# Attention slots: the value matmuls placed straight behind the second score pair

## The chip, the cores and the metric

The kernel runs on one core of a Trainium2 chip. The metric is device time in microseconds (us), the median of several executions; lower is better. TensorE (PE in the profile), VectorE (DVE), ScalarE (ACT), GpSimd (POOL) and the DMA queue of SyncE (SP) each take their own instructions in order; they meet at semaphores that the kernel sets and waits for by hand.

## The reference

`x` has 4 batches of 512 tokens of 128 channels. One transformer block with 16 heads of 8 channels, values equal to keys, and a mixture of 8 experts, of which each token takes 2:

```python
q = (x @ Wq + bq).reshape(B, N, H, Dh).transpose(0, 2, 1, 3)
k = (x @ Wk + bk).reshape(B, N, H, Dh).transpose(0, 2, 1, 3)
v = k
attn = jnp.einsum('bhnd,bhmd->bhnm', q, k) * scale
attn = jax.nn.softmax(attn, axis=-1)
out = jnp.einsum('bhnm,bhmd->bhnd', attn, v)
...
x = x + _L0_attn_ref(_layernorm(x, axis=-1), ...)
x = x + _L0_ffn_ref(_layernorm(x, axis=-1), ...)
```

## The kernel before

The four batches `b` go through one after the other. The attention of a batch is a loop over 16 slots `s`. A slot treats one group of four heads (`s // 4`) and one quarter of 128 keys (`s % 4`). After batches 1, 2 and 3 comes a loop over steps, one for each block of 128 expert rows (`up`, `gelu`, `down`); batches 1, 2 and 3 have a 17th slot for the last values.

Four kinds of work stand in TensorE's queue in a slot:

- `score_max` (L1066): one matmul of 512 columns that writes the scores of 128 queries of one head into one of two PSUM buffers, SM0 and SM1 in turn. VectorE takes their row maximum (`row_max`, L802). These maxima are made well ahead of the slot that uses them. A matmul of number m waits for the maximum of number m - 2, which read the same buffer (semaphore `sm_max`). A slot has 4 of them in batches 0 and 1 (5 in the first four slots, none from slot 11 of batch 1), 3 in batch 2, 2 in batch 3 up to slot 9. The steps have two each.
- `score_pair` (L1106): two matmuls into half of ST, which ScalarE turns into exponentials in `probs` (L699). A slot has two pairs. A pair waits for the exponentials of the pair before the last.
- `values` (L1118): four matmuls, one for each head, side by side on 32 columns of the array each, from `probs` of the slot before into AV. It waits for the exponentials of that slot, which the second pair has already waited for; at the first quarter of a group also for ScalarE's copy of AV (`av_done`, L691).
- a job in the PSUM buffer MISC (`fill_misc`): it waits until the job before it has been emptied (`misc_free`). Each engine that empties jobs has them at a fixed place of its own queue. VectorE empties x (turned input, L820), pr (projection, L778), q (turned queries, L797), out (turned attention output, L826 to L833), lg (logits) and rk (ranks); ScalarE empties k (turned keys), qr (turned queries with their row maxima, L603), x2 and xg (turned expert rows).

The jobs of the slots, apart from qr:

```python
0: {1: ("x", 1), 2: ("pr", 1, 0), 3: ("pr", 1, 1), 5: ("k", 1, 0), 6: ("out", 0, 0), 7: ("k", 1, 1),
    8: ("q", 1, 0), 9: ("q", 1, 1), 10: ("out", 0, 1), 14: ("out", 0, 2)},
1: {0: ("x", 2), 1: ("out", 0, 3), 2: ("pr", 2, 0), 3: ("x2", 0), 4: ("lg", 0), 5: ("pr", 2, 1), 6: ("rk", 0),
    8: ("out", 1, 0), 9: ("k", 2, 0), 10: ("out", 1, 1), 11: ("k", 2, 1), 12: ("q", 2, 0), 13: ("q", 2, 1),
    14: ("out", 1, 2), 15: ("xg", 0)},
2: {6: ("out", 2, 0), 10: ("out", 2, 1), 14: ("out", 2, 2), 15: ("xg", NQ)},
3: {6: ("out", 3, 0), 10: ("out", 3, 1), 14: ("out", 3, 2), 15: ("xg", 2 * NQ)},
```

The qr jobs are in slots 3, 7 and 11 of every batch and in slot 15 of batch 0: in batches 0 and 1 at the end of the slot, behind the last `score_max`, and in batches 2 and 3 ahead of the first pair.

VectorE's queue in a slot is: the first two row maxima, its part of the job, the other row maxima, and in some slots further work (layer norm moments and normalizing, choice of experts, `gate_weights`, `finish`), which stands at the end of the slot. ScalarE's is: the two exponentials, its part of the jobs, splitting of weights, the copy of AV.

Of the kernel before, what the change touches and what calls it, by code (L numbers as in the profile page):

```python
# [20 lines left out]
def preln_attention_moe(nc, x, wq, bq, wk, bk, w_gate, W1, b1, W2, b2, out):  # L21
# [3 lines left out]
    B, N, C = x.shape  # L25
    H, Dh = 16, C // 16
    E, _, F = W1.shape
    T = N // P
    G = H // 4
# [10 lines left out]
    with ExitStack() as ctx:  # L40
# [179 lines left out]
        def blocks_after(b):  # L220

            return range(0) if b == 0 else range(NB * (b - 1), NB * (b if b < B - 1 else B))

        def steps(b):

            return len(blocks_after(b)) + LAG if b else 0
# [21 lines left out]
        def slots(b):  # L248

            return range(4 * G if b == 0 else 4 * G + 1)  # L250

        def late_qr(b):

            return b <= 1
# [11 lines left out]
        def qr_of_slot(b, s):  # L266

            if s in QR:
                return ("qr", b, QR.index(s))
            if b == 0 and s == 4 * G - 1:  # L270
                return ("qr", 1, 0)
            return None

        def misc_of_slot(b, s):

            job, qr = IN_SLOT[b].get(s), qr_of_slot(b, s)
            return [j for j in ((job, qr) if late_qr(b) else (qr, job)) if j is not None]
# [744 lines left out]
        def _(pe):  # L1022
# [32 lines left out]
            def score_max(b, m):  # L1055

                if m % 32 == 0 or (b == 0 and m == LEAD):
                    pe.wait_ge(km_in[m // 32], 64 * (b + 1))
                if b == 0 and m == LEAD:
                    pe.wait_ge(qT_done, 2)  # L1060
                if b >= 1 and m % 32 == 0:
                    pe.wait_ge(misc_free, misc_no["q", b, m // 32] + 1)
                if SM_N * b + m >= LEAD + 2:
                    pe.wait_ge(sm_max, SM_N * b + m - 1)
                h = m // 4
                pe.matmul(SM[m % 2][:, :], qT0[:, b % 2, h // 4, P * (m % 4):P * (m % 4) + P], kTm[:, b % 2, h // 4, h % 4, :],  # L1066
                          start=True, stop=True).then_inc(sm_full, 1)
# [24 lines left out]
            def score_pair(b, s, pr):  # L1092

                g, c = s // 4, s % 4
                n = PAIRS * b + 2 * s + pr
                if n >= 2:
                    pe.wait_ge(exp_done, n - 1)
                if s == 0 and b >= 2:
                    if pr == 0:
                        pe.wait_ge(gelu_done, NB * (b - 1))  # L1100
                    else:
                        pe.wait_ge(yev_done, NQ * (b - 1))
                if c == 0:
                    pe.wait_ge(misc_free, misc_no["qr", b, g] + 1)
                for k in (2 * pr, 2 * pr + 1):
                    mm = pe.matmul(ST[:, n % 2, k % 2, :], kTm[:, b % 2, g, k, P * c:P * c + P], qT1[:, g % 2, :],  # L1106
                                   start=True, stop=True)
                mm.then_inc(st_full, 1)

            def values(u):  # L1110

                b, s = divmod(u, 4 * G)
                g, c = s // 4, s % 4
                if c == 0 and u >= 4:
                    pe.wait_ge(av_done, u // 4)
                pe.wait_ge(exp_done, 2 * u + 2)
                for j in range(4):
                    last = pe.matmul(AV[32 * j:32 * j + 32, :], v_aug[:, b % 2, c, 4 * g + j, :],  # L1118
                                     probs[:, (2 * u + j // 2) % 4, j % 2, :], start=(c == 0), stop=(c == T - 1))
                last.then_inc(av_step, 1)  # L1120
# [34 lines left out]
            def pick_expert(v):  # L1155

                f, j = v // NB, v % NB
                if j == 0:
                    pe.wait_ge(ex_done, f + 1)
                expert[v] = pe.value_load(exp_i[0:1, f, j:j + 1], min_val=0, max_val=E - 1)  # L1160

            def up(v):

                gq, j = group_of(v), v % NB % 4
                pe.wait_ge(w_in[v % RW], 16 * (v // RW + 1))
                if j == 0:
                    pe.wait_ge(misc_free, misc_no["xg", gq] + 1)
                if v >= 2:
                    pe.wait_ge(gelu_done, v - 1)
                dst, wb = UP[v % 2], wblk[:, v % RW, :]  # L1170
                pe.matmul(dst, wb[:, 2 * F:WB], sel[:, :, :].rearrange("p c n -> p (c n)"), start=True, stop=False)  # L1171
                for c in range(HC):
                    col = dst[:, P * c:P * c + P]
                    pe.matmul(col, wb[:, P * c:P * c + P], xgT[:, gq % 2, j, 0, :], start=False, stop=False)  # L1174
                    pe.matmul(col, wb[:, P * c:P * c + P], xgT[:, gq % 2, j, 1, :], start=False, stop=False)  # L1175
                    last = pe.matmul(col, wb[:, F + P * c:F + P * c + P], xgT[:, gq % 2, j, 0, :],  # L1176
                                     start=False, stop=(c == HC - 1))
                last.then_inc(up_full, 1)
# [29 lines left out]
            def fill_misc(job):  # L1208

                pe.wait_ge(misc_free, misc_no[job])  # L1210
                if job[0] == "x":
                    last = turn_x(job[1], MISC)
                if job[0] == "pr":
                    pe.wait_ge(misc_free, misc_no["x", job[1]] + 1)
                    project(2 * job[2], MISC)
                    last = project(2 * job[2] + 1, MISC)
                if job[0] == "k":
                    last = turn_k(job[1], job[2], MISC16)
                if job[0] == "q":
                    last = turn_q(job[1], job[2], MISC16)  # L1220
                if job[0] == "qr":
                    last = turn_qr(job[1], job[2])
                if job[0] == "out":
                    last = turn_out(job[1], job[2])
                if job[0] == "xg":
                    last = turn_xg(job[1])
                if job[0] == "x2":
                    last = turn_x2(job[1])
                if job[0] == "lg":
                    last = logits(job[1])  # L1230
                if job[0] == "rk":
                    last = rank_tokens(job[1])
                last.then_inc(misc_full, 1)
# [21 lines left out]
            for b in range(B):  # L1255
                for s in slots(b):
                    sm = sm_slot[b, s]
                    for bb, m in sm[0:1]:
                        score_max(bb, m)
                    if not late_qr(b) and s in QR:  # L1260
                        fill_misc(qr_of_slot(b, s))
                    if s < 4 * G:
                        score_pair(b, s, 0)
                    for bb, m in sm[1:2]:
                        score_max(bb, m)
                    if s < 4 * G:
                        score_pair(b, s, 1)
                    for bb, m in sm[2:3]:
                        score_max(bb, m)
                    for job in misc_of_slot(b, s):  # L1270
                        if job[0] != "qr":
                            fill_misc(job)
                    if s >= 1 or b == 1:
                        values(4 * G * b + s - 1)
                    for bb, m in sm[3:]:
                        score_max(bb, m)
                    if late_qr(b) and qr_of_slot(b, s) is not None:
                        fill_misc(qr_of_slot(b, s))
                todo = blocks_after(b)
                if b >= 1:  # L1280
                    pe.wait_ge(exp_done, PAIRS * (b + 1))
                for i in range(steps(b)):
                    for v in todo[i:i + 1]:
                        pick_expert(v)
                    sm = sm_step[b, i]
                    for bb, m in sm[0:1]:
                        score_max(bb, m)
                    for v in todo[i:i + 1]:
                        up(v)
                    for job in misc_of_step(b, i):  # L1290
                        fill_misc(job)
                    for bb, m in sm[1:2]:
                        score_max(bb, m)
                    if i >= LAG:
                        for v in todo[i - LAG:i - LAG + 1]:
                            down(v)
# [20 lines left out]
```

## Time and profile before

| what | value |
| --- | --- |
| median of 3 executions | 431.66 us (430.49 to 433.51) |
| the profiled execution | 433.75 us, its span 432.0 us |
| TensorE busy | 365.1 us, 85% of the span |
| VectorE busy | 251.6 us, 58% |
| ScalarE busy | 245.3 us, 57% |
| GpSimd busy | 124.5 us, 29% |
| slots of batches 0 and 1 | about 29 to 169 us of the span |
| slots of batch 2 | about 214 to 262 us |
| slots of batch 3 | about 303 to 344 us |

A matmul of 512 columns is shown with a duration of 0.38 us, but the next one can start 0.22 us after it; the duration holds the way through the array. The hardware profiler's times are of one execution; those of the table's first line are of three others.

### The profile page before, as it was taken

The numbers are of one execution on the slowest core, as the hardware profiler recorded it, in microseconds if no ns is written. First come the engines' busy times: TensorE is split into PE (matmuls) and PEld (weight loads), VectorE is DVE, ScalarE is ACT, GpSimd is POOL, SyncE is SP. The second block draws the span as 40 slices with busy tenths as digits, with TensorE's granted clock in tenths as the row PEclk, the third lists the DMA queues.
The fourth block names the chain that finished last, engine by engine and source line by source line (L and its number), as shares of the span: only waits on it lengthen the run. The fifth ranks groups of instructions, "written<-read, shape, count | busy, mean of one in ns | idle before, by whom it ended". The sixth has DMA issues, their size and how long they took to land. (4 is left out here: it accounts for less than half of the span.)

```text
span 432.0 us, 8187 instructions
## 1 busy us (share of the span) xinstructions
PE 365.1 (85%) x2858; PEld 203.3 (47%) x2858; DVE 251.6 (58%) x602; ACT 245.3 (57%) x322; POOL 124.5 (29%) x119
## 2 busy tenths in 40 slices
PE   6764998978787889899999799999899989899910
PEld 3311333322242334788723236788232379789910
DVE  5798777888878736875677877855555052000202
ACT  1423378786764778336487587333889944454410
POOL 5994112230041620203660000260420025107042
PEclk9655799999998999999999999999999999999975
DMA  5968002000000037232381001152720023576321
GB/s 169 313 174 247 2 0 50 1 2 0 27 0 0 31 101 252 85 135 67 113 275 44 24 2 57 56 189 73 231 92 24 2 112 138 168 256 222 114 78 49
DMA packets 43875, 42.92 MB, mean 99 GB/s; under 512 B 3314, under 2 KB 33082, under 8 KB 43836
## 3 DMA queue, kind: packets, MB, share of 16 engines
q1 hardware_dynamic: 41788, 38.20, 27.1%
q0 software_dynamic: 2048, 4.20, 3.3%
q8 instruction: 25, 0.41, 0.4%
q14 instruction: 14, 0.11, 0.1%
HBM read 11.58 MB, written 11.01 MB: 52 GB/s over the span
## 5 line engine op out<-in xcount | busy, mean ns | idle before, releaser
L802 DVE TENSOR_REDUCE q_aug<-SM 128x1 f16<-128x512 f32 x240 | 158.4, 689 | 52.3 <-PE SM L1066 50.6
L699 ACT ACTIVATE probs<-ST 128x1024 f32<-128x1024 f32 x128 | 124.7, 1023 | 53.0 <-PE ST L1106 52.4
L1066 PE MATMUL SM<-kTm,qT 128*128 128x512 f16 x240 | 93.7, 396 | 22.3 <-DVE q_aug L802 20.8
L1106 PE MATMUL ST<-qT,kTm 128*128 128x512 f16 x256 | 77.8, 392 | 7.2 <-ACT qT L603 4.4
L626 ACT ACTIVATE w<-ST 128x512 f32<-128x512 f32 x60 | 35.8, 597 | 77.5 <-PE ST L1176 76.1
L1118 PE MATMUL AV<-probs,v_aug 128*32 128x512 f32 x512 | 69.1, 614 | 0.3 <-ACT probs L699 0.3
L1066 PEld LDWEIGHTS SM<-kTm,qT 128*128 128x128 f16 x240 | 23.4, 99 | 97.3 <-DVE q_aug L802 72.2
L1192 PE MATMUL ST<-w 128*128 x480 | 66.6, 282 | 0.0
L1192 PEld LDWEIGHTS ST<-w 128*128 128x128 f32 x480 | 58.3, 192 | 3.1
L523 POOL DMA_INDIRECT w<-ys,pos x32 | 32.5, 1014 | 64.3 <-issue 44.5
L1175 PE MATMUL ST<-xgT,wblk 128*128 128x128 f16 x240 | 43.3, 219 | 0.0
L1174 PE MATMUL ST<-xgT,wblk 128*128 128x128 f16 x240 | 43.3, 219 | 0.0
L1176 PE MATMUL ST<-xgT,wblk 128*128 128x128 f16 x240 | 43.3, 219 | 0.0
L1106 PEld LDWEIGHTS ST<-qT,kTm 128*128 128x128 f16 x256 | 23.4, 100 | 38.2 <-ACT probs L699 14.3
L442 POOL TENSOR_TENSOR rstd<-ve,neg_half 128x4 f32<-128x4 f32 x8 | 8.2, 1031 | 113.4 <-DVE ve L759 113.3
L511 POOL DMA_INDIRECT xs<-x2s,pos x32 | 31.6, 989 | 22.5 <-DVE pos L884 13.6
L905 DVE SCALAR_TENSOR_TENSOR x<-w,wgt,x 128x128 f32<-128x128 f32 x16 | 4.5, 345 | 54.2 <-DMA w<-ys,pos 54.2
L1175 PEld LDWEIGHTS ST<-xgT,wblk 128*128 128x128 f16 x240 | 23.5, 98 | 7.1
L1174 PEld LDWEIGHTS ST<-xgT,wblk 128*128 128x128 f16 x240 | 23.5, 98 | 3.2
L1176 PEld LDWEIGHTS ST<-xgT,wblk 128*128 128x128 f16 x240 | 23.5, 98 | 0.0
L1171 PE MATMUL ST<-sel,wblk 128*128 128x512 f16 x60 | 22.7, 379 | 0.8 <-DMA wblk<-wpk 0.3
L1118 PEld LDWEIGHTS AV<-probs,v_aug 128*32 128x32 f32 x512 | 10.3, 109 | 19.2 <-issue 12.9
(146 smaller groups left out, 397.2 us busy)
## 6 DMA issues: line engine op xcount, KB each, us to landing
wblk<-wpk SPq DMA_DIRECT2D x60, 288.0 KB, 2.8
xs<-xg SPq DMA_DIRECT2D x4, 960.0 KB, 9.0
xg<-xs SPq DMA_DIRECT2D x12, 256.0 KB, 3.2
ys<-w SPq DMA_DIRECT2D x12, 256.0 KB, 2.3
w<-L_ffn_W SPq DMA_DIRECT2D x1, 2048.0 KB, 11.2
kTm<-kT SPq DMA_DIRECT2D x32, 64.0 KB
xt<-L_attn_x SPq DMA_DIRECT2D x4, 256.0 KB, 6.8
out<-x SPq DMA_DIRECT2D x4, 256.0 KB, 2.2
```

The source lines that it names most:

```text
L511: pool.indirect_dma_start(out=xs[b], out_offset=bass.IndirectOffsetOnAxis(ap=pos[:, b, r, t:t + 1], axis=0), in_=x2s[:, t, :, :].rearrange ...
L523: pool.indirect_dma_start(out=yg[:, t, r, :], out_offset=None, in_=ys[f], in_offset=bass.IndirectOffsetOnAxis(ap=pos[:, f, r, t:t + 1], ax ...
L626: act.activation(hf[:, v % HR, :], UP[v % 2], ACT.Gelu, scale=1.0 / WSCALE).then_inc(gelu_done, 1)
L699: act.activation(probs[:, n % 4, :, :], ST[:, n % 2, :, :], ACT.Exp, scale=SCALE).then_inc(exp_done, 1)
L802: dve.tensor_reduce(q_aug[:, b % 2, m % 4, m // 4, 24:25], SM[m % 2][:, :], AX.X, ALU.max, negate=True).then_inc(sm_max, 1)
L1066: pe.matmul(SM[m % 2][:, :], qT0[:, b % 2, h // 4, P * (m % 4):P * (m % 4) + P], kTm[:, b % 2, h // 4, h % 4, :], start=True, stop=True).t ...
L1106: mm = pe.matmul(ST[:, n % 2, k % 2, :], kTm[:, b % 2, g, k, P * c:P * c + P], qT1[:, g % 2, :], start=True, stop=True)
L1118: last = pe.matmul(AV[32 * j:32 * j + 32, :], v_aug[:, b % 2, c, 4 * g + j, :], probs[:, (2 * u + j // 2) % 4, j % 2, :], start=(c == 0), ...
L1174: pe.matmul(col, wb[:, P * c:P * c + P], xgT[:, gq % 2, j, 0, :], start=False, stop=False)
L1175: pe.matmul(col, wb[:, P * c:P * c + P], xgT[:, gq % 2, j, 1, :], start=False, stop=False)
L1176: last = pe.matmul(col, wb[:, F + P * c:F + P * c + P], xgT[:, gq % 2, j, 0, :], start=False, stop=(c == HC - 1))
L1192: last = pe.matmul(dst, hf[:, v % HR, P * c:P * c + P], w2[:, bass.ds(expert[v], 1), P * c:P * c + P].rearrange("p a n -> p (a n)"), start ...
```

## The change

In the slots, `values` is called straight behind the second `score_pair`, ahead of the third `score_max` and of the job. Nothing else is edited; waits, semaphores and the queues of the other engines stay as they are. In slots without a job it moves ahead of the third `score_max` alone; in batch 3, which has at most two, ahead of the job alone.

```diff
                     if s < 4 * G:
                         score_pair(b, s, 1)
+                    if s >= 1 or b == 1:
+                        values(4 * G * b + s - 1)
                     for bb, m in sm[2:3]:
                         score_max(bb, m)
                     for job in misc_of_slot(b, s):
                         if job[0] != "qr":
                             fill_misc(job)
-                    if s >= 1 or b == 1:
-                        values(4 * G * b + s - 1)
                     for bb, m in sm[3:]:
                         score_max(bb, m)
```

TensorE's queue in slot 9 of batch 0 (job q, `L1051`) and the first rows of slot 10, before:

```order
L1066 MATMUL SM0<-kTm,qT0 128x512
L1106 MATMUL ST<-qT1,kTm 128x512 x2
L1066 MATMUL SM1<-kTm,qT0 128x512
L1106 MATMUL ST<-qT1,kTm 128x512 x2
L1066 MATMUL SM0<-kTm,qT0 128x512
L1051 MATMUL MISC<-ident16,q_aug 128x128 x8
L1118 MATMUL AV<-probs,v_aug 32x512 x4
L1066 MATMUL SM1<-kTm,qT0 128x512
L1066 MATMUL SM0<-kTm,qT0 128x512
```

And the same place after the change:

```order
L1066 MATMUL SM0<-kTm,qT0 128x512
L1106 MATMUL ST<-qT1,kTm 128x512 x2
L1066 MATMUL SM1<-kTm,qT0 128x512
L1106 MATMUL ST<-qT1,kTm 128x512 x2
L1118 MATMUL AV<-probs,v_aug 32x512 x4
L1066 MATMUL SM0<-kTm,qT0 128x512
L1051 MATMUL MISC<-ident16,q_aug 128x128 x8
L1066 MATMUL SM1<-kTm,qT0 128x512
L1066 MATMUL SM0<-kTm,qT0 128x512
```

The values stood between the job and the fourth matmul into SM; now they stand between the second pair and the third, and the job is followed by the fourth.

TensorE's queue in slots 4 and 5 of batch 2 (three maxima, no job), before, from the second pair of slot 4 to that of slot 5:

```order
L1106 MATMUL ST<-qT1,kTm 128x512 x2
L1066 MATMUL SM0<-kTm,qT0 128x512
L1118 MATMUL AV<-probs,v_aug 32x512 x4
L1066 MATMUL SM1<-kTm,qT0 128x512
L1106 MATMUL ST<-qT1,kTm 128x512 x2
L1066 MATMUL SM0<-kTm,qT0 128x512
L1106 MATMUL ST<-qT1,kTm 128x512 x2
```

And after the change:

```order
L1106 MATMUL ST<-qT1,kTm 128x512 x2
L1118 MATMUL AV<-probs,v_aug 32x512 x4
L1066 MATMUL SM0<-kTm,qT0 128x512
L1066 MATMUL SM1<-kTm,qT0 128x512
L1106 MATMUL ST<-qT1,kTm 128x512 x2
L1066 MATMUL SM0<-kTm,qT0 128x512
L1106 MATMUL ST<-qT1,kTm 128x512 x2
```

The third matmul into SM, which stood ahead of the values, now stands directly ahead of the first of the next slot.

## Rows read from the trace of the kernel before

**Rows 1.** The page's costliest groups: busy, mean ns | idle before, releaser

```profile
L802 DVE TENSOR_REDUCE q_aug<-SM 128x1 f16<-128x512 f32 x240 | 158.4, 689 | 52.3 <-PE SM L1066 50.6
```

**Rows 2.** Time line, batch 0, from slot 10's second SM matmul: start us, us, engine, line

```profile
80.46 0.39 PE L1066 MATMUL SM<-kTm,qT 128*128 128x512 f16 x1
...
80.69 0.59 PE L1106 MATMUL ST<-qT,kTm 128*128 128x512 f16 x2
...
81.12 0.38 PE L1066 MATMUL SM<-kTm,qT 128*128 128x512 f16 x1
...
81.34 0.60 PE L1126 MATMUL MISC<-ident,avs 128*128 128x128 f32 x4
...
81.87 1.07 PE L1118 MATMUL AV<-probs,v_aug 128*32 128x512 f32 x8
81.97 0.26 DVE L826 RECIPROCAL rden<-MISC 128x16 f32<-128x16 f32 x1 [0.37 <-PE MISC L1126]
...
82.80 1.28 DVE L802 TENSOR_REDUCE q_aug<-SM 128x1 f16<-128x512 f32 x2
...
82.86 0.39 PE L1066 MATMUL SM<-kTm,qT 128*128 128x512 f16 x1
...
83.63 0.38 PE L1066 MATMUL SM<-kTm,qT 128*128 128x512 f16 x1 [0.38 <-DVE q_aug L802]
```

**Rows 3.** Time line, slots 12 and 13 of batch 0, no job

```profile
88.70 0.38 PE L1066 MATMUL SM<-kTm,qT 128*128 128x512 f16 x1
...
89.01 1.06 PE L1118 MATMUL AV<-probs,v_aug 128*32 128x512 f32 x8
...
90.01 0.61 PE L1066 MATMUL SM<-kTm,qT 128*128 128x512 f16 x2
...
90.44 1.29 DVE L802 TENSOR_REDUCE q_aug<-SM 128x1 f16<-128x512 f32 x2 [0.62 <-PE SM L1066]
...
91.19 0.39 PE L1066 MATMUL SM<-kTm,qT 128*128 128x512 f16 x1
```

**Rows 4.** Time line, batches 0 and 1, slots behind further work of VectorE

```profile
46.48 2.93 DVE L802 TENSOR_REDUCE q_aug<-SM 128x1 f16<-128x512 f32 x4 [1.11 <-PE SM L1066]
...
96.77 0.39 PE L1066 MATMUL SM<-kTm,qT 128*128 128x512 f16 x1 [1.62 <-DVE q_aug L802]
...
103.17 1.29 DVE L802 TENSOR_REDUCE q_aug<-SM 128x1 f16<-128x512 f32 x2 [0.61 <-PE SM L1066]
...
128.21 0.39 PE L1066 MATMUL SM<-kTm,qT 128*128 128x512 f16 x1 [0.47 <-DVE q_aug L802]
...
147.66 0.39 PE L1066 MATMUL SM<-kTm,qT 128*128 128x512 f16 x1 [0.36 <-DVE q_aug L802]
```

**Rows 5.** Time line, batch 2, slot 5, no job

```profile
228.69 0.38 PE L1066 MATMUL SM<-kTm,qT 128*128 128x512 f16 x1
...
229.34 0.38 PE L1066 MATMUL SM<-kTm,qT 128*128 128x512 f16 x1
...
231.30 0.38 PE L1066 MATMUL SM<-kTm,qT 128*128 128x512 f16 x1
```

**Rows 6.** Time line, batch 2, third matmul of slot 9 and second of slot 10

```profile
241.83 0.39 PE L1066 MATMUL SM<-kTm,qT 128*128 128x512 f16 x1 [1.21 <-DVE q_aug L802]
...
243.80 0.38 PE L1066 MATMUL SM<-kTm,qT 128*128 128x512 f16 x1
```

**Rows 7.** Time line, batch 3, out job of slot 6 and qr job of slot 7

```profile
319.58 0.60 PE L1126 MATMUL MISC<-ident,avs 128*128 128x128 f32 x4
...
320.51 0.29 DVE L828 TENSOR_TENSOR att<-MISC,rden 128x128 f32<-128x128 f32 x1
...
321.33 0.39 PE L1088 MATMUL MISC<-ident,q_aug 128*128 128x128 f16 x4
```

**Rows 8.** Time line, batch 1, slot 7, after VectorE's ranks

```profile
136.67 0.46 PE L1066 MATMUL SM<-kTm,qT 128*128 128x512 f16 x1 [2.56 <-DVE q_aug L802]
...
138.21 1.06 PE L1106 MATMUL ST<-qT,kTm 128*128 128x512 f16 x2
```

## The prediction

> **What bounds the kernel now.** I read the page's costliest groups first, then the time line of the slots, then the waits. On the page VectorE's row maxima (L802) are the largest group of the attention: 240 of 0.69 us, 158.4 us, and they stood idle 50.6 us for TensorE's matmuls of L1066 [rows 1]. Neither engine is full; they hand two SM buffers to and fro. So what matters is not how much TensorE does in a slot, which the change leaves alone, but how early in its queue the third maximum's matmul and the job stand.
>
> Slots 9 and 10 of batch 0 show the loop [rows 2]. The third row maximum of a slot has ended; then TensorE issues the next slot's first SM matmul, first pair, second SM matmul (80.46), second pair (80.69, two matmuls of 0.22 each, so until 81.12), third SM matmul at 81.12, the job at 81.34, the values at 81.87, the fourth SM matmul at 82.86. VectorE takes the job's result at 81.97, needs about 0.83 us for it, starts the third maximum at 82.80, and its end lets the next first matmul go at 83.63. VectorE was idle before 81.97: the slot's length runs through the second pair, the third matmul, the job, VectorE's part of the job and the third maximum. The values stand beside VectorE's work, in cover.
>
> **The price of the values ahead of the job.** From the start of one values group to the next matmul 1.00 us pass (89.01 to 90.01), and ahead of the first values matmul stands a hole of 0.09 (88.70 + 0.22 to 89.01) [rows 3]. The third matmul therefore comes 1.09 later behind the second pair. What that costs depends on the slot; counts are from the table of jobs.
>
> (a) Slots with a job that VectorE empties and four or five maxima: the whole 1.09, since job and third maximum both come later and the next first matmul waits for that maximum [rows 2]. The fourth matmul, freed earlier, doesn't help: its maximum stands behind the job on VectorE. These are slots 2, 3, 6, 8, 9, 10 of batch 0 and 0, 1, 4, 6, 8 of batch 1: 11 x 1.09 = **+12.0**.
>
> (b) Slots without a job, batch 0, slots 4, 12, 13. Before, the second matmul comes at 88.06 and again at 91.19: 3.13 apart [rows 3] (the first of these stands 0.64 before 88.70, as in rows 5). Now: second pair 88.27 to 88.70, values until 89.79, third matmul 89.79, fourth 90.01. A maximum starts 0.43 after its matmul (90.01 to 90.44) and takes 0.69, or 0.65 in a row: third maximum until 90.9, fourth until 91.55, next second matmul at 91.6. 3 x 0.42 = **+1.25**. Slot 5, whose job ScalarE empties (k), costs nothing by the same arithmetic: its fourth matmul stands behind pair, third, job and values in either order. Slot 7 has a k job and then a qr job that waits for ScalarE to empty it: ScalarE is free 0.5 us after the old k job is done, so about 0.58 of the 1.09 shows: **+0.6**. In slots 7 of batch 1 and 11 of batch 0 the qr job is behind the fourth matmul, and ScalarE's copy of it sets the end: 0.
>
> (c) Slots in which the third matmul waits anyway, since VectorE does other work at the end of the slot before. In slot 14 of batch 0 it waits 1.62 [rows 4], and the values fit in: 0 in place of 1.09. The same in slot 2 of batch 1. In slot 5 of batch 1 the wait is 0.47 [rows 4]; with the 0.16 by which a modelled end outlasts the issue of the next, 0.63 are covered, and 1.09 - 0.63 = **+0.5** is left. In four of these the fourth matmul stood behind the values with VectorE idle, and it now comes a microsecond sooner: slot 1 of batch 0 (idle 1.11) and slot 15 (idle 0.61 for its matmul; there the qr job behind it moves up by 0.9 with it) [rows 4], slot 3 of batch 1 (about 0.3, held by ScalarE's copy) and slot 9 of batch 1 (third matmul at 147.66 after a wait of 0.36, so the fourth comes half a microsecond sooner) [rows 4]: -1.1 - 0.9 - 0.3 - 0.55 = **-2.85**.
>
> (d) Batch 2, three maxima in a slot. TensorE is full: second matmul to second matmul 228.69 to 231.30, 2.61 [rows 5], and VectorE has slack. Now the third matmul stands at t behind the values, the next second matmul has to wait for its maximum (same buffer): t + 0.43 + 0.69 + 0.05 = t + 1.17, while TensorE would reach it at t + 0.22 + 0.22 + 0.43 = t + 0.87. So 0.30 in each of slots 1, 3, 4, 5, 7, 8, 11, 12, 13 (9 x 0.3 = 2.7), 0.08 in slot 2, where a qr job of 0.22 lies between. In slots 6, 10 and 14 the out job comes before the third maximum on VectorE: 0.79, 1.05 and 1.0. Slot 9 gains: its third matmul waits 1.21 at 241.83 and the values now fit ahead of it [rows 6]; the next second matmul follows its maximum at 243.0 in place of 243.8: -0.8. Together 2.7 + 0.1 + 2.85 - 0.8 = **+4.85**.
>
> (e) Batch 3, two maxima in a slot, so only the job moves. The out job of slot 6 goes from 319.58 to 320.67. VectorE frees MISC 1.22 us after the job's issue (320.51 + 0.29), and the qr job of slot 7 comes at 321.33 [rows 7]; it will wait until 320.67 + 1.27 = 321.94: 0.6. In slot 10 no row maximum lies between: 0.8. **+1.4**. The xg jobs of slot 15 and ScalarE's exponentials have cover: in slots 11 to 16 of batch 1 and in batch 3 I take 0.
>
> Outside the slots nothing is edited; all later stages start later by what has gathered, since TensorE takes them in order.
>
> **The sum.** 12.0 + 1.25 + 0.6 + 0.5 - 2.85 + 4.85 + 1.4 = +17.75 us. The profiled execution took 433.75 us (span 432.0), so 451.5 there; it was 2.1 above the median of 431.66, which gives **449.4**. About 1% (4.3 us) is what a measurement of this kernel can tell from no change.
>
> What is not shown by a row: how the fourth matmul, issued straight behind the job, and VectorE interleave in slots with five maxima, and ScalarE's copies (k, x2) coming later. From below these may take back 0.5 us in each of six slots, from above cost as much: +-3. Another unknown is that values of slots 5, 9 and 13 wait for ScalarE to copy AV (av_done); that copy ended 0.1 to 0.2 us before where the values now stand. It would cost at most 0.3 in each of 12 slots, and I take 0. The forecast's own range is 444 to 454.5.
>
> **The rivals.** *The clock.* In batch 1 TensorE waited 2.56 us for VectorE (at 136.67) and the matmuls behind it ran at the lower of its two levels: a pair took 1.06 us instead of 0.59 [rows 8]. In job slots TensorE will now idle some 1.3 us out of 4.7 where it idled 0.4 of 3.6. If that lowers the granted clock, TensorE's 3.3 us of a slot become 6.6, 1.9 more than the 4.7, in 11 slots: +21, near 470. Against it: around the waits of 1.62 [rows 4] pairs went on at full rate (the clock there was 1.00). [...] Chance 5%.
>
> *Most of it is hidden.* If VectorE's maxima of the fourth matmul could slip into the holes, or the 1.09 overlapped half with something I haven't seen, group (a) would cost 0.5 a slot: 449.4 - 6.5 = 443, and with (b) and (d) at nothing 439. For it speaks only that both engines have holes; against it, that each queue is in order. Chance 10%.
>
> *Faster.* The values ahead of a matmul that must wait fill TensorE's hole, as in the slots with a minus above. If job slots had the same wait (that is, if VectorE's second maximum rather than TensorE's place ended last), only the minuses would stand: -3.65, 428.0. It decides if the third matmul's wait for the first maximum is over 1.1 us in the usual slot; in [rows 2] that wait is nearly nothing (the matmul follows its pair by 0.43). Chance 3%, and within 1% by some mixture 2%.
>
> **How the numbers follow.** Forecast 80%, hidden 10%, clock 5%, faster or unchanged 5%. The forecast's range widened to the upper part of the hidden case and a little above gives 442 to 456, with some 15 to 20% outside. Slower by over 1%: 0.80 + 0.10 + 0.05 = 0.95; within 1%: 0.03; faster by over 1%: 0.02.
>
> **What would show it.** In the profile after: job slots of batch 0 of about 4.7 us from one third matmul to the next, for 3.6; VectorE idle about 1.4 before its part of an out or q job, where it was 0.4; its idle time for L1066 up from 50.6 and that ahead of jobs up by about a microsecond a slot; slots without a job 3.55; batch 2 at 2.9 for 2.61, its second matmul waiting 0.3 for VectorE; the row of slot 14 of batch 0 unchanged. I am wrong if job slots keep 3.6, or if the pairs of batch 0 take 1.06.

## The result, and the profile after

The changed kernel takes 454.34 us (median of 4, 453.50 to 457.26) for 432.39 of the kernel before: ratio 1.0515, 95% interval 1.0456 to 1.0574. The profiled execution took 457.26 with a span of 455.5, the longest of the four; the spans of the other three are 451.8 to 453.1. Ratios, here and below, leave out slow executions (one of twelve in each of two experiments, 436.70 and 901.81 us), which the medians hold.

The costliest groups on the page of the kernel after, the first answering to [rows 1]:

```profile
L802 DVE TENSOR_REDUCE q_aug<-SM 128x1 f16<-128x512 f32 x240 | 156.9, 688 | 57.1 <-PE SM L1066 55.4
L1066 PE MATMUL SM<-kTm,qT 128*128 128x512 f16 x240 | 92.8, 399 | 34.7 <-DVE q_aug L802 32.2
```

Every engine has the same instructions as before. TensorE is nevertheless busy for 374.1 us, where it was busy for 365.1: the same matmuls took longer in the mean (L1118 626 ns for 614, L1106 403 for 392), since more of them ran at the lower of its two clock levels, as shown further down. VectorE waits 4.8 us more for L1066. TensorE waits 32.2 us there, for 20.8 before. Most of VectorE's other new idle time is ahead of its jobs: ahead of the out jobs it waits 31.1 us for 21.4, ahead of pr 11.1 for 5.4, ahead of q 11.4 for 9.0. The time line of slot 9 of batch 0, to be held against [rows 2]:

```profile
82.61 0.38 PE L1066 MATMUL SM<-kTm,qT 128*128 128x512 f16 x1
...
82.82 0.59 PE L1106 MATMUL ST<-qT,kTm 128*128 128x512 f16 x2
83.35 1.06 PE L1118 MATMUL AV<-probs,v_aug 128*32 128x512 f32 x8
84.35 0.39 PE L1066 MATMUL SM<-kTm,qT 128*128 128x512 f16 x1
84.57 0.61 PE L1051 MATMUL MISC<-ident,q_aug 128*128 128x128 f16 x8
...
85.02 0.38 PE L1066 MATMUL SM<-kTm,qT 128*128 128x512 f16 x1
85.22 0.69 DVE L797 COPY qT<-MISC 128x1024 f16<-128x1024 f16 x1 [1.50 <-PE MISC L1051]
...
85.83 2.51 DVE L802 TENSOR_REDUCE q_aug<-SM 128x1 f16<-128x512 f32 x4
86.57 0.39 PE L1066 MATMUL SM<-kTm,qT 128*128 128x512 f16 x1 [1.17 <-DVE q_aug L802]
```

The reader is to see two holes that stand in for one another: VectorE is idle for 1.50 us until the job's result is there (0.37 before an out job in [rows 2]), and when it has copied it and made the third maximum, TensorE, idle for 1.17, gets its next first matmul. VectorE ends its last maximum at 83.72, so most of the values at 83.35 run while it has nothing to do but wait for the job behind them.

Batch 2 without a job, slots 4 and 5, against [rows 5]:

```profile
242.81 0.61 PE L1066 MATMUL SM<-kTm,qT 128*128 128x512 f16 x2
243.24 1.89 DVE L802 TENSOR_REDUCE q_aug<-SM 128x1 f16<-128x512 f32 x3 [0.41 <-PE SM L1066]
...
243.99 0.39 PE L1066 MATMUL SM<-kTm,qT 128*128 128x512 f16 x1
...
245.74 0.60 PE L1066 MATMUL SM<-kTm,qT 128*128 128x512 f16 x2
```

The third matmul (242.81) and the next slot's first follow the values; the next second matmul waits until 243.99, 1.18 after the third. A slot is 2.93 long for 2.61.

The table sets the forecast's groups against the profiled executions. A slot's length is the time from the start of its second pair to that of the next slot's, from the time lines; "measured" is after less before, in us.

| group of slots | forecast | measured |
| --- | --- | --- |
| (a) 11 slots with a job of VectorE | +12.0 | +14.4: eight of them 1.03 to 1.10, slot 8 of batch 1 1.19, slot 2 of batch 0 2.74, slot 4 of batch 1 1.91 |
| (b) slots 4, 5, 12, 13 of batch 0 | +1.25 | +1.27 |
| (b) slot 7 of batch 0 (k and qr) | +0.6 | +0.58 |
| (c) slots 14 (b 0), 2 and 5 (b 1) | +0.5 | -0.50, 0.00, +1.05 |
| (c) four slots with a gain | -2.85 | -1.45, -0.72, -0.32, -0.53 = -3.0 |
| (d) batch 2 | +4.85 | +7.7: ten plain ones 0.07 to 0.32, slots 6, 10, 14 0.91, 1.75, 1.10, slot 11 1.30 |
| (e) batch 3 | +1.4 | 0.68 + 0.90 + 0.05 = +1.6 |
| the other slots, the steps, ahead of slot 1, and the end | 0 | +0.4 |

### The profile page after: what moved, and what is told of

It reads as the page before. It is cut to its first block and busy times, and to the rows that moved or that the text cites. A ratio compares the mean times of both kernels' runs of the same rounds, so it can differ in the third digit from the quotient of the medians.

```text
span 455.5 us, 8187 instructions
## 1 busy us (share of the span) xinstructions
PE 374.1 (82%) x2858; PEld 202.2 (44%) x2858; DVE 248.5 (55%) x602; ACT 247.4 (54%) x322; POOL 124.5 (27%) x119
## 5 line engine op out<-in xcount | busy, mean ns | idle before, releaser
L1066 PE MATMUL SM<-kTm,qT 128*128 128x512 f16 x240 | 92.8, 399 | 34.7 <-DVE q_aug L802 32.2
L1106 PE MATMUL ST<-qT,kTm 128*128 128x512 f16 x256 | 80.3, 403 | 5.9 <-ACT qT L603 3.1
L1118 PE MATMUL AV<-probs,v_aug 128*32 128x512 f32 x512 | 70.8, 626 | 0.1
L1066 PEld LDWEIGHTS SM<-kTm,qT 128*128 128x128 f16 x240 | 22.9, 100 | 107.9 <-DVE q_aug L802 94.3
L1106 PEld LDWEIGHTS ST<-qT,kTm 128*128 128x128 f16 x256 | 24.1, 101 | 33.7 <-ACT probs L699 10.4
L511 POOL DMA_INDIRECT xs<-x2s,pos x32 | 31.6, 988 | 22.5 <-DVE pos L884 13.6
L905 DVE SCALAR_TENSOR_TENSOR x<-w,wgt,x 128x128 f32<-128x128 f32 x16 | 4.5, 346 | 55.7 <-DMA w<-ys,pos 55.7
L1175 PEld LDWEIGHTS ST<-xgT,wblk 128*128 128x128 f16 x240 | 23.5, 98 | 7.1
L1174 PEld LDWEIGHTS ST<-xgT,wblk 128*128 128x128 f16 x240 | 23.5, 98 | 3.0
L1176 PEld LDWEIGHTS ST<-xgT,wblk 128*128 128x128 f16 x240 | 23.5, 98 | 0.0
L1118 PEld LDWEIGHTS AV<-probs,v_aug 128*32 128x32 f32 x512 | 10.3, 110 | 28.5 <-issue 23.7
## 6 DMA issues: line engine op xcount, KB each, us to landing
w<-L_ffn_W SPq DMA_DIRECT2D x1, 2048.0 KB, 11.7
```

Of the source, the lines that this page charges most:

```text
L511: pool.indirect_dma_start(out=xs[b], out_offset=bass.IndirectOffsetOnAxis(ap=pos[:, b, r, t:t + 1], axis=0), in_=x2s[:, t, :, :].rearrange ...
```

## The experiments

Most edit the order in TensorE's part of a slot; two shorten the values, one adds matmuls, and two also change VectorE's order. "Cost", "gain" and "+" are the slot's length in the profiled execution less that of the kernel before; the columns of the rows are those of the time line. Times are medians, ratios are to runs of the kernel before on the same chip.

**The job late, the third maximum early.**

```diff
 (second score_pair, third score_max)
+values
 fill_misc(job)
```

> Half of the change: the third score_max stays ahead, only the job stands behind the values. If VectorE's part of the job is what comes late (my account), the 11 slots with a job that VectorE empties still cost 1.08 each (+11.9), batch 2 without a job costs nothing (2.61 a slot), slots of batch 0 without a job 3.14, the out slots of batches 2 and 3 about 1 each, and slots 14 of batch 0 and 2 of batch 1, where the values no longer fill a wait, lose 1.1 each: about 450. If it is the late third row maximum that costs, the job alone gives at most +4: 436.

Measured: 457.29 us, ratio 1.0589 (1.0536 to 1.0641). Ten of the eleven job slots cost 1.02 to 1.19 each (slot 2 of batch 0 1.71), about as with the whole change; batch 2 without a job is back at 2.61, batch 0 without one at 3.14. So the price of group (a) comes from the job's place: with the third matmul early it stays the same. The total is 7 over what I expected: slots in which the third matmul waits lose 1.14, 1.20, 1.12 and 0.57 (I had counted two of them, at 1.1 each), the gains of the five slots go, slots 2 and 3 lose 2.9 together, and slot 12 of batch 1 ran at the lower clock (+1.57).

**The third maximum late, the job first.**

```diff
 (second score_pair)
 fill_misc(job)
+values
 third and fourth score_max
```

> The other half, with the job first: second pair, job, values, third and fourth score_max. My account: job slots of VectorE 4.1 us (third maximum at 3.40 to 4.09 after the last third maximum, no longer held by the job) for 3.6 before and 4.65 with the change, +0.5 in 11 slots; slots without a job as with the change (3.57, batch 2 2.93): +5.5 +1.3 +3 and little else, about 443. If the job's place alone decides: 434. If both add up as in the change: 454.

Measured: 436.81 us, ratio 1.0112 (1.0061 to 1.0163). Job slots with a q job cost 0.43, out jobs 0.28, slots without a job 0.43 (batch 2: 0.32). In the time line of slot 9 the job is at once behind the pair, and VectorE waits 0.18 for it:

```profile
78.08 0.59 PE L1106 MATMUL ST<-qT,kTm 128*128 128x512 f16 x2
78.52 0.61 PE L1051 MATMUL MISC<-ident,q_aug 128*128 128x128 f16 x8
79.06 1.07 PE L1118 MATMUL AV<-probs,v_aug 128*32 128x512 f32 x8
79.16 0.69 DVE L797 COPY qT<-MISC 128x1024 f16<-128x1024 f16 x1 [0.18 <-PE MISC L1051]
...
80.05 0.60 PE L1066 MATMUL SM<-kTm,qT 128*128 128x512 f16 x2
```

It is 6 under my figure, because I missed what a job ahead of a waiting third matmul gives: slots 14 of batch 0 and 2, 3 and 6 of batch 1 are 0.92, 0.79, 0.89 and 1.12 shorter than before the change. Of the 1.12 in slot 6 some 0.67 is clock: the kernel before ran there at the lower level, and the run with five slots moved, which changes nothing in this slot, is 0.67 shorter too. The two halves, +25 and +4, don't add up to the change's +22; a likely place where they overlap is the slots with waits.

**The old place in the eleven job slots.**

```diff
+LATE = [(0, s) for s in (2, 3, 6, 8, 9, 10)] + [(1, s) for s in (0, 1, 4, 6, 8)]
 the changed kernel; values behind the job if (b, s) in LATE
```

> The changed kernel with the values back at their old place in the 11 slots of batches 0 and 1 whose job VectorE empties. My account: 11 x 1.08 come back, 454.3 - 11.9 = 442.4, and 440 if part of the stretches at the lower clock go with the holes. A rival in which the slots' prices don't add up (given back later, or set by the clock): 447 or more.

Measured: 442.68 us, ratio 1.0256 (1.0200 to 1.0313). 11.7 us come back. In the profiled execution nine of these slots have their length of before the change to 0.01, slot 6 of batch 1 is 0.30 shorter (at a clock higher than the kernel before had there), and slot 8 of batch 1 keeps the whole +1.19, although its values stand in the old place. There the excess isn't the price of the values. Its start in this kernel:

```profile
141.27 1.15 POOL L480 TENSOR_TENSOR q_aug<-qkf,q_aug 128x512 f16<-128x512 f32 x1 [7.25 <-ACT q_aug L585]
...
141.47 0.99 DVE L891 TENSOR_SCALAR exp_i<-exp_f 128x15 int32<-128x15 f32 x1
...
142.37 1.28 DVE L802 TENSOR_REDUCE q_aug<-SM 128x1 f16<-128x512 f32 x2
...
143.10 0.39 PE L1066 MATMUL SM<-kTm,qT 128*128 128x512 f16 x1 [1.05 <-DVE q_aug L802]
```

VectorE's L891, the last of slot 7's extra work, takes 0.99 us and ends with GpSimd's L480; the slot's maxima start as it ends, and the third matmul waits 1.05. In the changed kernel the same two instructions overlap, and the values fit into that wait:

```profile
155.99 1.16 POOL L480 TENSOR_TENSOR q_aug<-qkf,q_aug 128x512 f16<-128x512 f32 x1 [8.18 <-ACT q_aug L585]
...
156.18 0.99 DVE L891 TENSOR_SCALAR exp_i<-exp_f 128x15 int32<-128x15 f32 x1
...
156.71 1.06 PE L1118 MATMUL AV<-probs,v_aug 128*32 128x512 f32 x8
157.09 1.27 DVE L802 TENSOR_REDUCE q_aug<-SM 128x1 f16<-128x512 f32 x2
...
157.83 0.39 PE L1066 MATMUL SM<-kTm,qT 128*128 128x512 f16 x1
```

Before the change L891 took 0.17, at 142.57, and L480 began when it had ended, at 142.75. So the account of the job's place holds for ten of the eleven slots. In those the whole price came back, the low clock of slots 2 and 4 with it.

**Values of half the length, in the old and the new place.** In three of four slots the values matmuls cover 256 of 512 columns:

```diff
+w = N if c == 0 else N // 2
-AV[32 * j:32 * j + 32, :] ... probs[..., :]
+AV[32 * j:32 * j + 32, 0:w] ... probs[..., 0:w]
```

> The kernel before with the values matmuls of three quarters of the slots on 256 of 512 columns (half of the queries' weighted sums lack three of the four key quarters, so the output isn't the reference's). My account: in job slots of VectorE in batches 0 and 1 the values are in cover, so these keep 3.6 and 3.7; batch 2, batch 3 and the end of batch 1, where TensorE or ScalarE is full, fall by 0.4 a slot: about 421.

> The changed kernel with the same shortening (same part left out). My account: here the values stand on the path of job slots too, which fall by 0.43 from 4.62 to 4.2 (slots 2, 3, 6, 8, 10 of batch 0 and 0, 4, 6, 8 of batch 1): about 438, 17 above the shortened kernel with the old order, where the full ones are 22 apart. If the change's price doesn't hang on the length of the values (a fixed cost of the order or of the clock), the two stay 22 apart: 443.

Measured: 423.86 us (ratio 0.9807, 0.9739 to 0.9876) in the old place, 441.22 (1.0201, 1.0162 to 1.0240) in the new: 17.4 apart, for 21.95 with full values. In the old place job slots of batch 0 keep their length (3.59 to 3.52, out 3.73 and 3.81 unchanged): the values are in cover. In the new place slot 8 falls from 4.62 to 4.19 and slots 6 and 10 from 4.83 and 4.90 to 4.40 and 4.48. Slot 8 of that kernel:

```profile
77.95 0.64 PE L1119 MATMUL AV<-probs,v_aug 128*32 128x256 f32 x8
78.53 0.39 PE L1066 MATMUL SM<-kTm,qT 128*128 128x512 f16 x1
...
79.40 0.69 DVE L797 COPY qT<-MISC 128x1024 f16<-128x1024 f16 x1 [1.07 <-PE MISC L1051]
```

VectorE's wait is 1.07 where it was 1.50, shorter by 0.43; the values lost 0.42 (77.95 to 78.53 is 0.58 for 1.00). So the price of a job slot goes with the length of the values, as forecast: slot 8 costs 0.67 over the same slot in the old place (4.19 for 3.52), which is 0.58 and the hole of 0.09.

**Spare matmuls ahead of three long waits.**

```diff
+SPARE = {(1, 5), (1, 7), (2, 11)}
+for _ in range(2): the two matmuls of the slot's first pair, into the same buffer
```

> The changed kernel with four spare matmuls of 512 columns (the first pair of the slot, issued twice more than needed, into the same buffer that the pair then overwrites) ahead of the three longest waits of TensorE for VectorE: at the start of slots 5 and 7 of batch 1 and ahead of the qr job of slot 11 of batch 2. If the stretches at the lower clock behind these waits come from TensorE standing idle, they go, and the time falls by 2 to 3 us to 451.5; the granted clock of those stretches is 1.00. If the clock falls whatever stands there, or my price per slot was too low instead, the time stays at 454 or rises by up to 1.

Measured: 452.54 us, ratio 1.0482 (1.0424 to 1.0539), for 1.0515 of the changed kernel: the intervals overlap, so the medians alone show no gain. The profiled executions (span 450.5 for 455.5) show what differed. In the changed kernel TensorE waited 1.87 us in slot 5 of batch 1 and 2.08 in slot 11 of batch 2, and the pairs behind took 1.06:

```profile
136.67 0.61 PE L1066 MATMUL SM<-kTm,qT 128*128 128x512 f16 x1 [1.87 <-DVE q_aug L802]
137.07 1.06 PE L1106 MATMUL ST<-qT,kTm 128*128 128x512 f16 x2
...
265.90 0.44 PE L1088 MATMUL MISC<-ident,q_aug 128*128 128x128 f16 x4 [2.08 <-DVE q_aug L802]
266.14 1.06 PE L1106 MATMUL ST<-qT,kTm 128*128 128x512 f16 x2
```

With the spare matmuls, which shorten the two waits by 0.86 us, the same places:

```profile
137.40 0.39 PE L1066 MATMUL SM<-kTm,qT 128*128 128x512 f16 x1 [1.01 <-DVE q_aug L802]
137.63 0.59 PE L1106 MATMUL ST<-qT,kTm 128*128 128x512 f16 x2
...
263.48 0.38 PE L1088 MATMUL MISC<-ident,q_aug 128*128 128x128 f16 x4 [1.22 <-DVE q_aug L802]
263.70 0.59 PE L1106 MATMUL ST<-qT,kTm 128*128 128x512 f16 x2
```

The stretch of 261 to 272 us, by windows (span, busy times, then PEclk), in the changed kernel and then with the spare ones:

```profile
261.00:272.00 11.00, 8.78 (x46) 2.78 (x49) 5.54 (x11) 5.38 (x7) 0.00 (x0) 0.84 0.00 0
```

```profile
261.00:272.00 11.00, 9.50 (x56) 2.77 (x55) 6.51 (x12) 7.00 (x8) 0.00 (x0) 1.00 0.01 1
```

Slots 4 to 7 of batch 1 are 3.1 us shorter together and 10 and 11 of batch 2 1.6. Slot 4 of batch 1 falls from 1.91 over the kernel before to 1.10, slot 5 from 1.05 to 0.39, slot 10 of batch 2 from 1.75 to 1.10 and slot 11 from 1.30 to 0.32: the forecast's prices, once the clock is out of them.

That the spare matmuls kept the clock up isn't shown. The same waits, without any spare matmul, were also followed by the full clock in other profiles: 1.87 in slot 5 of batch 1 with the job late and with half values in the new place, and 2.08 in slot 11 of batch 2 with the latter:

```profile
258.70 0.38 PE L1088 MATMUL MISC<-ident,q_aug 128*128 128x128 f16 x4 [2.08 <-DVE q_aug L802]
258.92 0.59 PE L1106 MATMUL ST<-qT,kTm 128*128 128x512 f16 x2
```

Only at the third place, slot 7 of batch 1, do the profiles point one way: the wait of 3.52 was followed by the lower level in all three profiles that have it, and the 2.66 left with spare matmuls was not.

**Only five slots moved.**

```diff
+EARLY = {(0, 1), (0, 15), (1, 3), (1, 9), (2, 9)}
 the kernel before; values ahead of the third score_max if (b, s) in EARLY
```

> The kernel before, with the values moved only in slots 1 and 15 of batch 0, 3 and 9 of batch 1 and 9 of batch 2, where they fill a wait of TensorE or free the fourth matmul. My account: -1.1 -0.9 -0.3 -0.5 -0.8, 3.6 us under the kernel before, ratio 0.992. If these gains were only slack of the slower loop: ratio 1.000.

Measured: 429.39 us, ratio 0.9950 (0.9917 to 0.9983). The profiled slots show -2.26 in slot 1, -0.72 in slot 15, -0.33 and -0.53 in batch 1, and -0.72 in slot 9 of batch 2, where the whole change gave +0.07. The gains are real. In the medians they come to 2.5 us rather than 3.6, and the interval just reaches 3.6. The -2.26 isn't the price of the order alone: the kernel before ran slot 1 at the lower clock (its values took 1.94 us), this one at the full clock from 42 us on. In slots 6 and 7 of batch 1 the clock alone gives -1.6, in slots 11 and 12 +1.6.

**Values behind the fourth score_max.**

```diff
 third score_max, fill_misc(job), sm[3:]
+values
 late qr job
```

> The opposite move: values behind the fourth score_max, ahead of a late qr job. If the hand-over of SM and MISC sets the slot and the values only fill, job slots stay at 3.6, slots with a k job fall by 0.3, slot 1 of batch 0 by 1.1: ratio 0.995. If the exponentials need the values early (probs comes free late), slower, 1.01.

Measured: 436.37 us, ratio 1.0096 (1.0070 to 1.0122). Wrong on my side: in slots 1 to 3 of batch 0 the values stand behind a fifth matmul that waits for the third maximum, behind the job (+0.98, +1.41, +1.10; in the first two part of it is the lower clock, in slot 3 the fifth matmul waits 1.17), and a qr job behind the values costs 0.31 and 0.38 in slots 11 and 15. Slot 14 gained 1.17, and slot 12 of batch 1 ran at the lower clock (+1.62). The job slots of batch 0 from 6 on stay at 3.5 to 3.8, as expected.

**The same, and VectorE takes the third maximum ahead of the job.**

```diff
-for bb, m in sm[0:2]: row_max      # VectorE
+for bb, m in sm[0:3]: row_max
 empty_misc(job)
```

> As the one before, and VectorE takes the third row maximum ahead of its part of the job. My account: VectorE has then no hole ahead of the job, job slots fall from 3.6 to 3.3, out slots from 3.8 to 3.5: 3 us more, ratio 0.988. If MISC coming free 0.65 later holds qr jobs or the next job, nothing is gained: 0.995 or more.

Measured: 424.30 us, ratio 0.9825 (0.9792 to 0.9858), a larger gain than the 0.988 I expected. Slots 6, 8, 9 and 10 of batch 0 are 3.27 long for 3.6 to 3.8; there VectorE has no hole ahead of the job:

```profile
77.48 0.60 PE L1126 MATMUL MISC<-ident,avs 128*128 128x128 f32 x4
77.92 0.38 PE L1066 MATMUL SM<-kTm,qT 128*128 128x512 f16 x1
78.23 1.07 PE L1118 MATMUL AV<-probs,v_aug 128*32 128x512 f32 x8
78.29 0.25 DVE L826 RECIPROCAL rden<-MISC 128x16 f32<-128x16 f32 x1
```

**The job first, the values last**, with a lone qr job ahead of them, and early only in slots 15 of batch 0 and 9 of batch 2; VectorE's order as before in the first kernel, third maximum first in the second.

```diff
 (second score_pair)
+fill_misc(job)
 sm[2:4], qr job if alone
+values
 sm[4:], qr job otherwise
```

> A version from the findings: the job stands first behind the second pair, then the third and fourth score_max, a qr job where the slot has no other, the values, and the fifth score_max; only in slots 15 of batch 0 and 9 of batch 2 the values stay ahead of the third score_max. VectorE's order is that of the kernel before. My account: VectorE gets the job when its second maximum ends, job slots 3.3 for 3.6, slots whose third matmul waits lose 0.8 to 1.1 each as in the run with the job first: 421, ratio 0.976. If the values behind everything hold the next slot's first matmul instead: 0.99.

> The same with VectorE taking the third maximum ahead of the job. If the job's result is there when the second maximum ends, this order gains nothing over the one above (0 in job slots) and in slots whose third matmul waits it puts the job behind that wait: +0.7 in five slots, 424.5, ratio 0.983. If the next slot's first matmul, which needs the third maximum, sets the slot, it gains 0.2 a slot: 419.

Measured: 423.03 us, ratio 0.9779 (0.9753 to 0.9805), and 424.02, ratio 0.9812 (0.9785 to 0.9840). The first has the lowest median of all runs, 8.6 under the kernel before on the same chip (431.64) and 31.3 under the changed one; its interval overlaps those of the two other good versions, so the three are not told apart.

## Why the prediction was right, and where it was short

The forecast was 449.4 us with a range of 444 to 454.5; 454.34 lies 0.2 under the upper end. The mechanism is borne out slot by slot. The sum is short, and what it lacks is named below.

**The path in a job slot** (second pair, third matmul, job, VectorE's part, third maximum) and its price of 1.09 were right: eight slots measure 1.07 in the mean (8.52 together), half-length values cut the price of slot 8 to 0.67, the length left to them and the hole, and the old place in eleven slots returned 11.7 us. Slot 8 of batch 1 came to the forecast's size by luck: its 1.19 is the long L891 and what follows from it, not the place of its values.

**Slots without a job**, of batch 0 (0.42 forecast, 0.43 measured) and batch 2 (0.30 and 0.32) were right, and so were the jobs of batch 3 (0.6 and 0.8 forecast, 0.68 and 0.90 measured). The run with only the job late shows that the price of the slots without a job comes from the third maximum: there it is gone.

**Waits that the values fill.** Three of the four gains of batches 0 and 1 came about as worked out (-0.72, -0.32 and -0.53 for -0.9, -0.3 and -0.55); the run with five slots moved shows them without the rest. The fourth, slot 1 of batch 0, agrees (-1.45 for -1.1) by luck. The idle 1.11 us of [rows 4] it was read from stands in a stretch at the lower clock: TensorE's granted clock was 0.50 from 38 to 46 us of the kernel before, and the values of that slot took 1.94 us for 1.06. The changed kernel ran the middle of this slot at the full clock and its end at the lower. The same order in slot 1 gave -0.42 in the run with spare matmuls (which stand far behind it) and -2.26 in two others, so no single number is its price. Slot 14 of batch 0 gained 0.50 that I had not counted: VectorE's L759 took 0.62 us there before the change, beside GpSimd's L486, and 0.17 after it. It is the case of L891 with the other sign; the 0.45 between the two is nearly all of the gain.

**The step that failed** is the last of (d): "Slot 9 gains ... -0.8". It measures +0.07. I treated VectorE's `finish` as fixed in time, but it stands in VectorE's queue behind the third maximum of slot 8, which the change makes later. From slot 8's second pair to `finish` (L905) it took 1.45 us before (237.41 to 238.86) and takes 2.56 now (254.26 to 256.82), 1.11 more:

```profile
255.78 0.61 PE L1066 MATMUL SM<-kTm,qT 128*128 128x512 f16 x2
...
256.82 1.13 DVE L905 SCALAR_TENSOR_TENSOR x<-w,wgt,x 128x128 f32<-128x128 f32 x4
...
259.79 0.39 PE L1066 MATMUL SM<-kTm,qT 128*128 128x512 f16 x1 [1.00 <-DVE q_aug L802]
```

So slot 9's third matmul still waits 1.00 us behind its values. With slot 8 left in the old order, slot 9 did gain 0.72.

**The clock** is what I had at 5%, as a state of all job slots, and otherwise at nothing. It came in another form. Nearly all job slots keep the full clock in their holes of 1.17 us; but longer waits of TensorE, which the change lengthens, were followed by stretches at the lower level: 0.81 + 0.66 us in slots 4 and 5 of batch 1 and 0.65 + 0.98 in slots 10 and 11 of batch 2 (changed kernel less the one with spare matmuls). Slot 2 of batch 0, 1.65 over its price, ran in such a stretch too, behind waits of no more than 1.58 and 1.17 us:

```profile
47.30 1.06 PE L1106 MATMUL ST<-qT,kTm 128*128 128x512 f16 x2
```

The profiled span grew by 23.5 us for a forecast of 17.75, 5.75 more. The low clock makes 3.1 of it in those four slots and 1.65 in slot 2, slot 9 of batch 2 0.87; that is 5.6. Of the small parts that are left, slot 14 is the largest with -0.5. In the median the miss is 4.9 us (454.3 for 449.4), of which 0.7 is the kernel before, whose median came out at 432.39 for the 431.66 that the forecast started from. The stretches differ between profiles even where nothing ahead of them was edited, so how much of the median they hold isn't settled; the spare matmuls took 1.8 us off it, within the intervals. That waits bring the stretches about is likely and not shown.

## What to carry to other kernels

Independent work that fills an engine's queue belongs behind the last instruction that another engine waits for, not ahead of it: here the same 1.00 us of matmuls was in cover at one place and cost 1.07 a slot ahead of the third matmul and the job, with the same instructions on every engine. It doesn't belong behind an instruction that must itself wait either: behind the waiting fifth matmul the values cost 1.10 in slot 3. Before moving it, list for each slot which instruction of the other engine ends last, and let everything that stands behind it in that engine's queue move with it. Where two engines hand buffers to and fro, their orders are one problem: job first on TensorE, or the third maximum first on VectorE, gave 2%, where moving the values alone gave half a per cent at best.

## What the runs showed of the hardware

TensorE fell to the lower of its two clock levels (pairs of 1.06 us for 0.59) behind waits of 1.87, 2.08 and 3.52 us in the changed kernel and of 2.56 in the kernel before. In other profiles the same waits were followed by the full clock: 1.87 twice, 2.08 once, and 2.56 in slot 7 of batch 1 in two runs (five slots moved, values behind the fourth); so was one of 2.98 with half values in the old place. Waits of 1.17 us in a row of job slots and the 1.62 of [rows 4] were not followed by it, but slot 2 of batch 0 of the changed kernel fell behind waits of 1.58 and 1.17, soon after a longer stretch at the lower level. The length of the last wait alone, then, doesn't tell the level. The same place differs between kernels and executions: slot 12 of batch 1, 2.41 long in both kernels compared, took 3.7 to 4.0 in the profiles of five experiments and 3.0 to 3.2 in two more.

A small VectorE instruction can last as long as a large GpSimd one beside it. L891 (128x15) took 0.17 us in eight profiles and 0.99 to 1.18 in the five in which GpSimd's L480 (128x512) had started just before it; L759 (128x4) in slot 14 of batch 0 took 0.24 to 0.87 in the five in which it started while L486 ran, and 0.17 in the other eight. Each time both ended within 0.05 us of one another:

```profile
94.94 1.15 POOL L486 TENSOR_TENSOR wpk<-w,wpk 128x512 f16<-128x512 f32 x1 [2.33 <-ACT wpk L656]
...
95.50 0.62 DVE L759 TENSOR_SCALAR ve<-mv 128x4 f32<-128x4 f32 x1
```

That is the kernel before: 94.94 + 1.15 = 96.09, 95.50 + 0.62 = 96.12. For the pair of L480 and L891 the ends are 157.15 and 157.17 in the changed kernel, 142.42 and 142.46 with the old place in eleven slots. Not every GpSimd instruction does this: beside L511, a DMA instruction that had started 0.1 us before it, a later L891 took 0.17 or 0.18 in all thirteen profiles. The Trainium skill, page SBUF — State Buffer, section Who interferes with whom, says that a tensor_scalar in a two-port mode and a GpSimd instruction hold the same pair of ports as a lock, so that the second stands until the first has ended; these ends agree with it, though no run here moved one of the two alone, and no row tells which mode L891 and L759 were in. A shift of a few tenths of a microsecond between engines thus decides up to a microsecond, and none of it can be seen in a count of instructions.
